# The last batch's products in another order, and its first quarter scaled on another engine

## The reference

```python
memory_proj = jnp.einsum('bme,de->bmd', memory, W_mem)
scores = jnp.einsum('bnd,bmd->bnm', hidden_states, memory_proj) / jnp.sqrt(jnp.float32(D))
attn = jax.nn.softmax(scores, axis=-1)
memory_context = jnp.einsum('bnm,bmd->bnd', attn, memory_proj)
gate_input = jnp.concatenate([hidden_states, memory_context], axis=-1)
gate = jax.nn.sigmoid(jnp.einsum('bnf,df->bnd', gate_input, W_gate) + b_gate)
fused = hidden_states + gate * memory_context
var = jnp.mean(jnp.square(fused), axis=-1, keepdims=True)
out = fused * jax.lax.rsqrt(var + 1e-06) * norm_w
```

## Time and profile before

| what | value |
|---|---|
| time, median of 3 runs | 918.56 us (917.84 to 919.24) |
| profiled execution, its own time | 917.03 us |
| its span, first to last instruction | 915.3 us |
| busy in the span: PE, PEld | 906.0 us (99%), 764.6 us (84%) |
| busy in the span: DVE, ACT, POOL | 750.8 us (82%), 425.0 us (46%), 54.3 us (6%) |
| chain that ended last, by engine | PE 98%, DVE 1%, others 0% each |
| mean granted TensorE clock | 0.997 |

### The profile page before, as it was taken

How to read it: one execution, slowest core, us unless ns; L and a number is a source line. 1 busy time by engine, 2 the same in 40 slices (tenths; PEclk the granted TensorE clock), 3 DMA queues, 4 the chain that set the end, 5 groups by cost and what they waited for, 6 DMA issues and landing times.

```text
span 915.3 us, 11754 instructions
## 1 busy us (share of the span) xinstructions
PE 906.0 (99%) x4380; PEld 764.6 (84%) x4380; DVE 750.8 (82%) x963; ACT 425.0 (46%) x633; POOL 54.3 (6%) x73
## 2 busy tenths in 40 slices
PE   9999999999999999999999999999999999999996
PEld 8888888888888888888888888888888888888885
DVE  6997667767767989789796598888888988898887
ACT  6432222322232554554555465555555555555553
POOL 0000000000000000000000011110011111111102
PEclk9999999999999999999999999999999999999998
DMA  9323356556454665786879935455555545444542
GB/s 317 119 93 139 92 184 214 222 193 229 176 169 142 242 230 167 270 304 219 299 250 389 373 114 184 161 192 208 207 207 189 202 163 178 171 170 172 207 184 92
DMA packets 56504, 183.74 MB, mean 201 GB/s; under 512 B 5632, under 2 KB 13568, under 8 KB 50944
## 3 DMA queue, kind: packets, MB, share of 16 engines
q1 hardware_dynamic: 56160, 182.47, 55.9%
q10 hardware_dynamic: 288, 0.52, 0.2%
HBM read 127.93 MB, written 55.05 MB: 200 GB/s over the span
## 4 chain that ended last, share of the span: by engine, by line
PE 98%; DVE 1%; POOL 0%; ACT 0%; issue 0%; DVEq 0%; POOLq 0%
PE psum L1592 32%; PE psum L1593 32%; PE psum L1594 32%; PE psum L1694 1%; PE psum L1599 1%; DVE xlast L1585 0%; DVE zb L1509 0%; DVE zb L1467 0%; DVE mem L1452 0%; PE psum L1610 0%; POOL stat L666 0%; PE psum L1618 0%; PE psum L1614 0%; POOL stat L662 0%; ACT zb L941 0%
## 5 line engine op out<-in xcount | busy, mean ns | idle before, releaser
L1592 PE MATMUL psum<-g1h,xh 128*128 128x512 f32 x416 | 161.8, 389 | 0.0
L1593 PE MATMUL psum<-g_l,xh 128*128 128x512 f32 x416 | 161.8, 389 | 0.0
L1592 PEld LDWEIGHTS psum<-g1h,xh 128*128 128x128 f32 x416 | 78.1, 188 | 16.5 <-issue 0.2
L1593 PEld LDWEIGHTS psum<-g_l,xh 128*128 128x128 f32 x416 | 78.1, 188 | 16.3
L1467 DVE TENSOR_TENSOR zb<-psum,zb 128x512 f32<-128x512 f32 x112 | 76.7, 685 | 16.1 <-PE psum L1594 16.1
L1594 PE MATMUL psum<-g1h,xs_l 128*128 128x512 f32 x192 | 74.7, 389 | 0.0
L673 ACT ACTIVATE xh<-xs_raw 128x512 fp32r<-128x512 f32 x48 | 30.3, 632 | 95.5 <-PE psum L1594 95.5
L648 POOL TENSOR_TENSOR stat<-stat 128x1 f32<-128x1 f32 x30 | 19.7, 658 | 842.4 <-ACT zb L929 842.4
L1592 PE MATMUL psum<-yh,ws_h 128*128 128x512 f32 x160 | 62.5, 390 | 0.0
L1594 PE MATMUL psum<-yh,ws_l 128*128 128x512 f32 x160 | 62.3, 389 | 0.0
L1186 DVE TENSOR_TENSOR z<-psum,bias 128x512 f32<-128x512 f32 x48 | 33.1, 691 | 29.6 <-PE psum L1594 29.6
(11 more groups left out here) (200 smaller groups left out, 2511.0 us busy)
## 6 DMA issues: line engine op xcount, KB each, us to landing
b_raw<-in_xt SPq DMA_DIRECT2D x32, 512.0 KB, 7.8
zb<-z_spill SPq DMA_DIRECT2D x16, 1024.0 KB, 6.3
xrow<-in_x SPq DMA_DIRECT2D x30, 512.0 KB, 6.2
out<-xrow SPq DMA_DIRECT2D x30, 512.0 KB, 3.9
xs_raw<-in_xt SPq DMA_DIRECT2D x12, 1024.0 KB, 4.8
z_spill<-z SPq DMA_DIRECT2D x12, 1024.0 KB, 8.4
y_spill<-y SPq DMA_DIRECT2D x40, 256.0 KB, 3.7
yt_raw<-y_spill SPq DMA_DIRECT2D x16, 512.0 KB, 3.5
```

What stands on the lines that cost most here:

```text
L1592: nc.tensor.matmul(tile, ah, mh, start=start, stop=False, skip_group_check=True)
L1593: nc.tensor.matmul(tile, ah, ml, start=False, stop=False, skip_group_check=True)
```

## The change

In the last batch only:

- The quarters' order is changed: the second quarter is now (row block 0, columns 512 up), the third (row block 1, columns 512 up). The first and the last are as before. So row block 0 has both its quarters first.
- To feed them in that order, product 5 is done ahead of product 4 (`LAST_ORDER`), and the counts that the waits use are computed by `made`.
- z sum 4 now stands directly behind the second quarter's gate times context, ahead of its sum with x.
- The first quarter is also multiplied by norm_w early (a second `f_norm`, in the place of its context), and ACT scales it by rstd (`scale_quarter(0)`), between the squares of the third and the fourth quarter. DVE's last scalings are two in place of three.
- POOL makes rstd of row block 0 after the second quarter's square, and rstd of row block 1 from its own sum of the third quarter and DVE's sum of the fourth.

Shown below is the order on three engines. In the names, `wb0_..` and `wb1_..` are the right-hand factors of the mem half and the gate half, and the digit behind is the product; `zb1` is z of the last batch, `mem` its context, `xlast` its x and then its result; `stat` holds the columns of sums and rstd.

The diff:

```diff
--- before.py
+++ after.py
@@ -160,7 +160,7 @@
         xrow = at("xrow", [PART, NB, D], F32, 89)
 
         xlast = at("xlast", [PART, NB, D], F32, 149)
-        f_norm = mem[:, 1, 0:BANK]
+        f_norm = {0: mem[:, 0, 0:BANK], 3: mem[:, 1, 0:BANK]}
         zb = [at(f"zb{p}", [PART, NB, D], F32, (97, 9)[p]) for p in range(2)]
 
         rowmax, negmax = stat[:, 0:2], stat[:, 2:4]
@@ -345,7 +345,14 @@
         Y_LAST = P7 * SB
 
 
-        QUARTERS = [(0, 0), (1, 1), (0, 1), (1, 0)]
+
+        QUARTERS = [(0, 0), (0, 1), (1, 1), (1, 0)]
+        LAST_ORDER = (0, 1, 2, 3, 5, 4, 6)
+
+        def made(b, i):
+
+            return P7 * b + (LAST_ORDER.index(i) if b == B - 1 else i) + 1
+
 
         Y_SUM = {T1: 1, T2: 2, T4: 3}
 
@@ -625,9 +632,12 @@
                     sp.wait_ge(t_mm, 2 * (b + 2))
                     sp.dma_start(c_raw[:, :, :], c[b + 2]).then_inc(c_in, DMA)
 
-            for n, q in enumerate((0, 2, 1)):
+            for q in range(3):
                 nb, h = QUARTERS[q]
-                sp.wait_ge(row_done, 2 * (B - 1) + n + 1)
+                if q == 0:
+                    sp.wait_ge(q_scaled, 1)
+                else:
+                    sp.wait_ge(row_done, 2 * (B - 1) + q)
                 sp.dma_start(out[B - 1][:, nb, HALF[h]], xlast[:, nb, HALF[h]]).then_inc(out_done[nb], DMA)
             for nb in range(NB):
                 sp.wait_ge(out_done[nb], DMA * (B + 1))
@@ -654,17 +664,18 @@
                 for nb in range(NB):
                     root(b, nb)
 
+            pool.wait_ge(sq_q, 1)
+            pool.tensor_tensor(guarded[:, 0:1], part[:, 0:1], eps, ALU.add).then_inc(guarded_done, 1)
             pool.wait_ge(sq_q, 2)
-            for nb in range(NB):
-                pool.tensor_tensor(guarded[:, nb:nb + 1], part[:, nb:nb + 1], eps, ALU.add).then_inc(guarded_done, 1)
+            pool.wait_ge(guarded_done, 2 * B - 1)
+            pool.tensor_tensor(guarded[:, 0:1], part[:, 1:2], guarded[:, 0:1], ALU.add).then_inc(guarded_done, 1)
+            pool.wait_ge(guarded_done, 2 * B)
+            pool.tensor_tensor(rstd[:, 0:1], guarded[:, 0:1], minus_half, ALU.pow).then_inc(rstd_done, 1)
             pool.wait_ge(sq_q, 3)
-            pool.wait_ge(guarded_done, 2 * B)
-            pool.tensor_tensor(guarded[:, 0:1], part[:, 2:3], guarded[:, 0:1], ALU.add).then_inc(guarded_done, 1)
-
-            for nb in range(NB):
-                pool.wait_ge(guarded_done, 2 * B + 1 + nb)
-                pool.tensor_tensor(rstd[:, nb:nb + 1], guarded[:, nb:nb + 1], minus_half, ALU.pow
-                                   ).then_inc(rstd_done, 1)
+            pool.tensor_tensor(guarded[:, 1:2], part[:, 2:3], eps, ALU.add).then_inc(guarded_done, 1)
+
+            pool.wait_ge(guarded_done, 2 * B + 2)
+            pool.tensor_tensor(rstd[:, 1:2], guarded[:, 1:2], minus_half, ALU.pow).then_inc(rstd_done, 1)
 
 
         @block.scalar
@@ -931,7 +942,7 @@
 
             def tanh_quarter(q):
                 nb, h = QUARTERS[q]
-                act.wait_ge(z_done, P7 * (B - 1) + (2, 5, 6, 7)[q])
+                act.wait_ge(z_done, made(B - 1, (1, 5, 4, 6)[q]))
                 quarter = zb[(B - 1) % 2][:, nb, HALF[h]]
                 nc.scalar.activation(quarter, quarter, ACT.Tanh, scale=0.5).then_inc(tanh_q, 1)
 
@@ -940,6 +951,14 @@
                 act.wait_ge(f_q, q + 1)
                 nc.scalar.activation(zb[(B - 1) % 2][:, nb, HALF[h]], xlast[:, nb, HALF[h]], ACT.Square, scale=SCALE,
                                      accum_out=part[:, q:q + 1]).then_inc(sq_q, 1)
+
+            def scale_quarter(q):
+
+                nb, h = QUARTERS[q]
+                act.wait_ge(fn_done, {0: 1, 3: 2}[q])
+                act.wait_ge(rstd_done, 2 * (B - 1) + nb + 1)
+                nc.scalar.activation(xlast[:, nb, HALF[h]], f_norm[q], ACT.Copy, scale=rstd[:, nb:nb + 1]
+                                     ).then_inc(q_scaled, 1)
 
             t_cuts_high(0)
             for b in range(B):
@@ -977,13 +996,11 @@
                     tanh_quarter(2)
                     tanh_quarter(3)
                     square_quarter(2)
+                    scale_quarter(0)
                     square_quarter(3)
+                    scale_quarter(3)
                     nb, h = QUARTERS[3]
-                    act.wait_ge(fn_done, 1)
-                    act.wait_ge(rstd_done, 2 * B)
-                    nc.scalar.activation(xlast[:, nb, HALF[h]], f_norm, ACT.Copy, scale=rstd[:, nb:nb + 1]
-                                         ).then_inc(q_scaled, 1)
-                    act.wait_ge(q_scaled, 1)
+                    act.wait_ge(q_scaled, 2)
                     act.dma_start(out[B - 1][:, nb, HALF[h]], xlast[:, nb, HALF[h]]).then_inc(out_done[nb], DMA)
 
 
@@ -1447,7 +1464,7 @@
                 p = b % 2
                 dst, bk, copied, added = {1: (mem[:, 0, HALF[0]], 1 - p, 1, 1), 4: (mem[:, 1, HALF[1]], p, 3, 2),
                                           5: (mem[:, 0, HALF[1]], 1 - p, 2, 3)}[i]
-                dve.wait_ge(mem_mm, P7 * b + i + 1)
+                dve.wait_ge(mem_mm, made(b, i))
                 dve.wait_ge(mem_copied, 4 * b + copied)
                 nc.vector.tensor_tensor(dst, bank(bk), dst, ALU.add).then_inc(mem_added, 1)
 
@@ -1459,10 +1476,11 @@
                                   2: (zp[:, 0, HALF[1]], chain, 0), 3: (zp[:, 1, HALF[1]], other, 0),
                                   4: (zp[:, 1, HALF[1]], chain, 4), 5: (zp[:, 0, HALF[1]], other, 3),
                                   6: (zp[:, 1, HALF[0]], chain, 0)}[i]
-                dve.wait_ge(gate_mm, P7 * b + i + 1)
+                dve.wait_ge(gate_mm, made(b, i))
                 if i == 0:
                     dve.wait_ge(zb_in[p], DMA * (b // 2 + 1))
                 if after:
+
                     dve.wait_ge(z_done, P7 * b + after)
                 nc.vector.tensor_tensor(dst, bank(bk), dst, ALU.add).then_inc(z_done, 1)
 
@@ -1499,7 +1517,7 @@
                 gate, row = zb[b % 2][:, nb, HALF[h]], xlast[:, nb, HALF[h]]
                 dve.wait_ge(tanh_q, q + 1)
                 if q < 3:
-                    dve.wait_ge(mem_copied, 4 * b + (1, 3, 2)[q])
+                    dve.wait_ge(mem_copied, 4 * b + (1, 2, 3)[q])
                     dve.wait_ge(mem_added, 3 * b + (1, 2, 3)[q])
                     context = mem[:, nb, HALF[h]]
                 else:
@@ -1510,13 +1528,16 @@
                 dve.wait_ge(gm_q, q + 1)
                 if q == 0:
                     dve.wait_ge(xlast_in, DMA)
+                elif q == 1:
+
+                    z_out(b, 4)
                 elif q == 2:
                     z_out(b, 6)
                 nc.vector.scalar_tensor_tensor(row, gate, 0.5, row, ALU.mult, ALU.add).then_inc(f_q, 1)
-                if q == 3:
+                if q in (0, 3):
 
                     dve.wait_ge(f_q, q + 1)
-                    nc.vector.tensor_tensor(f_norm, row, norm[:, HALF[h]], ALU.mult).then_inc(fn_done, 1)
+                    nc.vector.tensor_tensor(f_norm[q], row, norm[:, HALF[h]], ALU.mult).then_inc(fn_done, 1)
 
             t_first(0)
             t_second(0)
@@ -1544,8 +1565,8 @@
                     yt_cut(b + 2)
                 if b == B - 1:
                     fuse_quarter(0)
-                    z_out(b, 4)
-                    mem_add(b, 4)
+                    z_out(b, 5)
+                    mem_add(b, 5)
                 else:
                     mem_add(b, 4)
                     z_out(b, 4)
@@ -1557,8 +1578,7 @@
                     ct_cut(b + 2)
                 if b == B - 1:
                     fuse_quarter(1)
-                    z_out(b, 5)
-                    mem_add(b, 5)
+                    mem_add(b, 4)
                 else:
                     mem_add(b, 5)
                     z_out(b, 5)
@@ -1578,7 +1598,7 @@
             dve.wait_ge(guarded_done, 2 * B + 1)
             nc.vector.tensor_tensor(guarded[:, 1:2], part[:, 3:4], guarded[:, 1:2], ALU.add).then_inc(guarded_done, 1)
 
-            for q in (0, 2, 1):
+            for q in (1, 2):
                 nb, h = QUARTERS[q]
                 dve.wait_ge(rstd_done, 2 * (B - 1) + nb + 1)
                 row = xlast[:, nb, HALF[h]]
@@ -1765,7 +1785,13 @@
                             pe.wait_ge(wb0_low, 2)
                             pe.wait_ge(y_added, 6 * SB)
                             pe.wait_ge(y_copied, 8 * SB)
-                    if m == 0:
+                    if b == B - 1 and i in (4, 5):
+
+                        if m == 0:
+                            pe.wait_ge(mem_copied, 4 * b + {5: 3, 4: 2}[i])
+                        else:
+                            pe.wait_ge(z_done, made(b, {5: 3, 4: 2}[i]))
+                    elif m == 0:
                         if i == 0 and b >= 1:
                             pe.wait_ge(mem_added, 3 * b)
                         elif i == 1 and b >= 1:
@@ -1773,14 +1799,14 @@
                         elif i in (2, 4, 5):
```

(8 more changed lines are left out.)

## The result

| | before | changed |
|---|---|---|
| median of 22 runs each | 918.26 us (917.31 to 920.63) | 919.63 us (918.49 to 922.36) |
| ratio to before | 1 | 1.0016, 95% interval 1.0010 to 1.0022 |
| span of the profiled execution | 915.3 us | 917.5 us |

A forecast was written before the change was run, and what follows sets the result against it. PE matmuls bound the kernel up to 901.6 us, then a chain led by DVE; z sum 6 comes 1.72 later, the shortened end leaves +1.25, so 918.56 + 1.25 = 919.8 us, range 918.8 to 920.9.

The forecast's parts named there:

- PE stops for 1.13: Last batch, fifth place: product 5's gate half waits for DVE to read its bank, making later PE work 1.13 us later.
- DVE and ACT stepped through by spacings: Last batch: starts listed by measured spacings put z sum 6 at 907.69, 1.72 us behind, and the small add at 911.28.
- Where the other 1.15 come from: Delay at z sum 6 beyond the PE stop's 0.57: added norm product (0.73) and the tanh behind a waiting square.
- ACT's scaling is hidden: First quarter's scaling on ACT, between the last two squares, costs nothing: ends 910.48, square due 910.53, cover 0.05.
- Rival 3: ACT becomes the bound: late scaling of the first quarter pushes the last square and the end; 920.5 us, chance 0.16.
- The power is held: POOL's last power waits for DVE's second-quarter scaling and ends at 912.52; without this the sum is about 0.5 less.
- Rival 1: POOL's last power isn't held by DVE's scaling and ends at 912.04; 0.5 less, 919.3 us, chance 0.13.
- The end: Last scalings and DMAs: +1.32 by issues alone, +1.24 with the transfers, taken as 1.25 us.
- the base of 918.56: Median of the runs before the change, to which the forecast added its step of 1.25 us.
- Rival 4: Shorter end wins: small add to last issue 2.09 held or 1.6 free, against 2.49; 917.9 us, chance 0.04.

The follow-up runs named there:

- the kernel with both edits: Changed kernel, with product 5's mem half first and the third quarter's tanh ahead of the second's square; end 16.41 from z sum 3, execution 921.44 us.

## Why the prediction was right

By its steps:

- *PE stops for 1.13.* The release was mis-sized: the first matmul started 0.15 behind the end of z sum 3, not 0.24, and so came 1.04 late (0.84 against -0.20). But it took 0.47 in place of 0.39, and the next ones stood 0.30 and 0.23 to 0.24 behind, which together is 0.09 more than the forecast's spacings, so that the mem sum of that place was late by 1.13 after all. That the two errors cancel to the hundredth is luck. What would be won back without the stop, forecast 0.57, is 0.53 to 0.56 with the mem half first.
- *DVE and ACT stepped through by spacings.* From the norm product to the small add all within 0.03. z sum 4, for which I kept 0.82 open because of its three waits, stood 0.73 behind gate times context.
- *Where the other 1.15 come from.* Here the prediction was wrong, though its times were right. It put 0.73 on the norm product. Two kernels without it have z sum 6 in the same place (8.74 and 7.61). In the changed kernel mem sum 5 waits for PE in any case, and with product 5's mem half first z sum 5 does, so the product is done while DVE would be idle. Read along the changed kernel's own path, the 1.70 are PE's 1.13 at mem sum 5 (3.85 against 2.72) and the 0.57 of the tanh behind the square. Of the 1.13, the mem half first gives back 0.53, and 0.60 stay with the order: before, the mem sum started at 2.72 as PE's last input came; in the order with product 5 and without the stop, z sum 5 takes that place, and the mem sum is one DVE instruction later (3.32 to 3.33). From the mem sum to z sum 6 it is 4.30 before and 4.29 without the stop, the late tanh and the norm product, so nothing is lost behind it. The split holds for these edits in this order; on the kernel before, where PE was in time, the same norm product cost 0.53. Moving mem sum 4 by one place gives back 0.19 of the 0.60 (7.62 to 7.43). The prediction's own list held the 902.80 that mem sum 5 waits for; it only failed to ask, of each DVE instruction in front of it, whether its removal would move anything.
- *ACT's scaling is hidden.* It ended at 911.37 and the last square started at 911.55, as DVE released it: cover 0.18, where 0.05 was forecast. The scaling began when the square had run its 0.63 (910.03 to 910.66), before the read of its sum was over (910.57 + 0.19), where the forecast had counted 0.72 for both. That square starts 0.73 behind the sum with x, as before. Rival 3 fell.
- *The power is held.* Ended 0.40 behind DVE's scaling, 13.54 against 13.57, and the run with the power first shows that it is DVE's scaling and not that the power stands alone. Rival 1 fell. Its price, forecast 0.5, wasn't measured by itself: the run with the power first gains 0.44 at ACT's scaling and 0.24 at the end, but it also starts DVE's scaling 0.20 later, and with it the second quarter's transfer.
- *The end.* By issues +1.32 forecast, +1.29 measured; with the transfers +1.24 forecast, +1.16 in the profile; the medians differ by 1.37, which the runs' scatter allows. The total, 919.8 against 919.63, is closer than its parts: the base of 918.56, from 3 runs, was 0.30 above the median of 22, and the step 0.12 too small. That is luck as well.
- *Rival 4.* From the small add to the last issue 2.08 against 2.49: that gain is real (0.41), and smaller than the 1.70 lost ahead of it.

What stays open: why PE's first matmul after a stop takes 0.47 and the second starts 0.30 behind it. The length of the stop doesn't matter in these rows (0.47 behind stops of 0.23, 0.30, 0.88 and 1.68 us); no run here varies anything else.

## What to carry to other kernels

In a relay of short instructions, list every start with measured spacings, and mark what sets it; then the cost of an added instruction is not its length but what it is to the next marked wait: 0 in front of a long enough wait for PE, and 0.53 of its 0.73 where that wait was 0.18. Before products are reordered, look at which PSUM bank each adds to: two in a row on one bank make PE wait for the reader between them (0.88 idle here), and doing the other half first takes that hole away, at the price of a later z sum. In an engine's own queue, what waits for a later result (here a square) should not stand ahead of what the chain needs next (a tanh).

## What the runs showed of the hardware

A power on POOL of one column takes 0.55 when it starts 0.04 ahead of a DVE instruction with two SBUF inputs, and 0.99 when it starts 0.16 behind that one's start; it then ends 0.40 behind the DVE instruction. The DVE instruction isn't held in turn: two scalings take 1.41 from 0.04 behind the power's start, and three take 2.07 where DVE was first, 0.66 for one more, so none of them waited for the power. Beside a z sum, which has one of its inputs in PSUM, the power took 0.55 even though DVE had begun 0.20 earlier (897.64 and 897.44 in the changed kernel). The same 0.99 came in all kernels where DVE was first, also where a second scaling followed at once: the power got in between the two. A tiny DVE instruction and a wait in front of the scaling, together 0.20, brought the power's end forward by 0.44.

The single executions reached the last batch between 898.95 and 903.29 us with the same code before it, and loads are the part of this that the chains show, at the start and near 525 us: in the slowest (the kernel with both edits) the load of `c_raw` took 11.53 us where it stands on the chain, PE stood still for 1.68 at 528, and did 526 matmuls between 500 and 600 us where the kernel before did 538.
